# Cross-attention in a decoder layer: how the turned probabilities get from one SBUF tile to another

## The reference

```
h_q = (rmsnorm(layernorm(x)) @ w_q.T).reshape(b, lq, H, DH)
h_k = (ctx @ w_k.T).reshape(b, lk, H, DH)
h_v = (ctx @ w_v.T).reshape(b, lk, H, DH)
score = einsum('bqhd,bkhd->bhqk', h_q, h_k) + position_bias[None]
score = softmax(where(mask, score, -inf)); score = where(mask, score, 0)
attn = einsum('bhqk,bkhd->bqhd', score, h_v).reshape(b, lq, H * DH)
x = layernorm(x)-part + attn @ w_out.T + residual
```

## Time and profile before

| what | value |
|---|---|
| time, median of 3 runs | 1894.92 us |
| the profiled execution's own time | 1894.83 us |
| its span (first to last instruction) | 1893.0 us |
| TensorE busy | 1859.4 us, 98% |
| VectorE, ScalarE, GpSimd busy | 1332.1, 1030.4, 1083.5 us |
| granted clock of TensorE, mean | 0.993 |
| store of xturned, 61 issues | 256 KB each |
| loads of xpraw, 244 issues | 64 KB each |

### The profile page before, as it was taken

One profiled execution on the slowest core, in us unless ns is written; L12 is line 12 of the kernel. 1 busy time (PEld: TensorE's weight loads), 2 busy tenths in 40 slices (PEclk: granted clock), 3 DMA queues, 4 the chain that ended last, 5 costly groups with the idle time before them and its releaser, 6 DMA issues.

```text
span 1893.0 us, 32031 instructions
## 1 busy us (share of the span) xinstructions
PE 1859.4 (98%) x9902; PEld 1598.2 (84%) x9902; DVE 1332.1 (70%) x2212; ACT 1030.4 (54%) x2265; POOL 1083.5 (57%) x861
## 2 busy tenths in 40 slices
PE   9899999999999999998999999999999999999998
PEld 6788888888888888876888888888888888888887
DVE  7688888888888888867666676666666766766132
ACT  3566666666666666655444444444444444445443
POOL 3788888888888888772443443333434434424643
PEclk9999999999999999998999999999999999999999
DMA  7555555555555555641222222222222222212332
GB/s 256 129 126 127 127 127 129 124 127 127 126 128 126 126 126 126 156 128 47 93 87 85 78 83 91 83 70 75 86 91 86 85 85 80 70 55 80 100 121 74
DMA packets 142282, 201.03 MB, mean 106 GB/s; under 512 B 29714, under 2 KB 67218, under 8 KB 141714
## 3 DMA queue, kind: packets, MB, share of 16 engines
q1 hardware_dynamic: 142226, 200.33, 38.0%
HBM read 98.25 MB, written 18.09 MB: 61 GB/s over the span
## 4 chain that ended last, share of the span: by engine, by line
PE 93%; DVE 3%; ACT 2%; issue 1%; SPq 1%; POOL 1%; DMA 0%; DVEq 0%; ACTq 0%
PE bank L1391 25%; PE bank L1392 25%; PE bank L1393 25%; PE bank L1471 11%; PE bank L1616 2%; PE bank L1617 2%; PE bank L1663 2%; PE bank L1664 2%; PE bank L1461 1%; DVE negmax L1012 1%; SPq L295 1%; DVE probT L1020 0%; DVE xacc L1031 0%; ACT prob L657 0%; PE bank L1412 0%
## 5 line engine op out<-in xcount | busy, mean ns | idle before, releaser
L490 POOL TENSOR_TENSOR pT_lo<-pT_lo,pT_hi 128x512 fp32r<-128x512 f32 x320 | 406.3, 1296 | 112.4 <-ACT pT_hi L598 112.4
L1031 DVE SCALAR_TENSOR_TENSOR xacc<-bank,rinv,xacc 128x512 f32<-128x512 f32 x504 | 364.0, 733 | 5.4 <-PE bank L1393 5.4
L657 ACT ACTIVATE prob<-bank,negmax 128x640 f32<-128x640 f32 x256 | 204.0, 797 | 253.1 <-DVE negmax L1012 252.2
L1020 DVE STREAM_TRANSPOSE probT<-prob 128x640 f32<-128x640 f32 x256 | 214.6, 838 | 108.7 <-ACT prob L657 108.7
L1012 DVE TENSOR_REDUCE negmax<-bank 128x1 f32<-128x640 f32 x256 | 207.3, 810 | 39.8 <-PE bank L1471 31.5
L473 POOL TENSOR_TENSOR xwo_lo<-xwo_raw,xwo_hi 128x512 fp32r<-128x512 f32 x32 | 41.5, 1298 | 268.4 <-ACT xwo_hi L598 268.4
L598 ACT ACTIVATE pT_hi<-pT_lo 128x512 fp32r<-128x512 f32 x320 | 185.6, 622 | 3.9 <-DMA pT_lo<-probT 3.9
L473 POOL TENSOR_TENSOR xwq_lo<-xwq_raw,xwq_hi 128x512 fp32r<-128x512 f32 x32 | 41.6, 1299 | 236.5 <-ACT xwq_hi L598 236.5
L1391 PE MATMUL bank<-wx_hi,cT_hi 128*128 128x256 f32 x512 | 142.2, 278 | 1.2 <-DVE xk L1140 1.2
L1393 PE MATMUL bank<-wx_hi,cT_lo 128*128 128x256 f32 x512 | 142.0, 277 | 0.0
L1392 PE MATMUL bank<-wx_lo,cT_hi 128*128 128x256 f32 x512 | 141.9, 277 | 0.0
(11 more groups left out here) (202 smaller groups left out, 5549.1 us busy)
## 6 DMA issues: line engine op xcount, KB each, us to landing
pT_lo<-probT SPq DMA_DIRECT2D x1024, 80.0 KB, 2.1
w_raw<-in_w SPq DMA_DIRECT2D x64, 256.0 KB, 2.8
xturned<-xturn SPq DMA_DIRECT2D x61, 256.0 KB, 2.0
xpraw<-xturned SPq DMA_DIRECT2D x244, 64.0 KB, 2.0
wx_raw<-in_wq SPq DMA_DIRECT2D x32, 256.0 KB, 2.6
wo_raw<-in_wo SPq DMA_DIRECT2D x32, 256.0 KB, 2.7
wx_raw<-in_xwv SPq DMA_DIRECT2D x16, 512.0 KB, 3.3
xwk_raw<-in_xwk SPq DMA_DIRECT2D x32, 256.0 KB, 2.8
```

Of the source, the lines that this page charges most:

```text
L490: g.tensor_tensor(tile, tile.bitcast(F32), four(pT_hi[:, j, :]), ALU.subtract).then_inc(a["pTlo"], 1)
L657: s.activation(prob[:, i % 2, :].rearrange("p (a t) -> p a t", a=2), S_bank[i % 2], ACT.Exp, bias=negmax[:, u % 2, i:i + 1], scale=1.0, ac ...
L1020: v.transpose(probT[:, u % 2, :, :, i * 32:(i + 1) * 32], prob[:, i % 2, :].rearrange("p (t j n) -> p j t n", j=4, n=32)).then_inc(a["turn ...
L1031: v.scalar_tensor_tensor(xacc[:, 4 * half + i, :], M, rinv[:, k, i:i + 1], xacc[:, 4 * half + i, :], ALU.mult, ALU.add).then_inc(sems["y"], 1)
```

## The change

In `c_turn` the store to device memory, the wait for it and the four loads are replaced by 16 transfers straight from xturn to xpraw, one for each block (i, j): 32 partitions, 128 floats (512 bytes) on each. Each adds 16 to the semaphore, so ScalarE waits for 256 (TURN) per unit instead of 64. VectorE, before it overwrites a slot of xturn, waits for the landing of that slot's 16 transfers, where it waited for the store.

```
 def c_turn(it, u):
-    n, use = it * 4 + u, it * 2 + (u + 1) // 2
+    n = it * 4 + u
     sp.wait_ge(c["turned"], n)
     if not isinstance(n, int) or n > 2:
         sp.wait_ge(c["pTlo"], n - 1)
-    sp.dma_start(xturned[u % 2], xturn[:, u % 2].rearrange("p j b q -> p (j b q)")).then_inc(s_xst[u % 2], 16)
-    sp.wait_ge(s_xst[u % 2], use * 16)
-    for j in range(4):
-        sp.dma_start(xpraw[j * 32:(j + 1) * 32, u % 2].rearrange("p i b q -> p i (b q)"),
-                     xturned[u % 2].rearrange("(i k) (j n) -> k i j n", i=4, j=4)[:, :, j, :])\
-          .then_inc(s_xpT[u % 2], 16)
+    for i in range(4):
+        for j in range(4):
+            sp.dma_start(xpraw[j * 32:(j + 1) * 32, u % 2, i],
+                         xturn[i * 32:(i + 1) * 32, u % 2, j]).then_inc(s_xpT[u % 2], 16)
...
 # ScalarE, c_step
-    act.wait_ge(s_xpT[u % 2], (it * 2 + (u + 1) // 2) * 64)
+    act.wait_ge(s_xpT[u % 2], (it * 2 + (u + 1) // 2) * TURN)
...
 # VectorE, c_step
-    dve.wait_ge(s_xst[1 - k], (it * 2 + u // 2) * 16)
+    dve.wait_ge(s_xpT[1 - k], (it * 2 + u // 2) * TURN)
```

## The result

The changed kernel takes 1995.64 us, the median of 3 runs (1994.32 to 1999.83), against 1894.92: a ratio of 1.054, 95% interval 1.052 to 1.056, or +100.7 us. The forecast was 2009 us, slower.

The account below looks back on a forecast made before the run. TensorE, full throughout steady cross-attention, bounds the kernel; afterwards the issue-to-issue loop would: 60 x 14.57 + 30 x 0.49 = 888.9 us against 775.0, +113.9 on 1894.8, taken as 2009 us; overall range 1922 to 2045.

Parts of the forecast that it names:

- The price of an issue: SyncE's queue: 0.59 us per SBUF-to-SBUF transfer, as in the self-attention; last of 16 starts 9.42 us after the first.
- Rivals (1): SyncE issues at the pitch of device-memory loads, 0.48 us: +28, 1923 us; chance 0.10 with prices between.
- (2): Not slower: SyncE issues short rows at 0.35 us or less, TensorE covers it, 1895 us; chance 0.07.
- The landing: Time from a transfer's issue to its data in xpraw: 2.1 us, so data lands 11.5 us after the first issue.
- list of signs: Profile signs; wrong if the set takes under 9 us, landing is not 2.1, or 14.6 us pacing lacks +110 us.
- ring (b): Wait ring through one landing and TensorE's value products: 56.1 us in four units, against 51.92 for TensorE alone.
- (a): Loop between successive sets' first issues, through landing, copy, exponentials and VectorE: 59.3 us in four units, the longest.
- TensorE's idle time: TensorE before the value product, mostly units 1 and 2: about 110 us idle in sum, granted clock still 1.00.
- rival (3): TensorE's clock falls after idle gaps; 5 us of work lost after each of two gives +213, 2108 us; chance 0.05.
- What was costed at nothing: Saved device-memory traffic, VectorE's wait for the landing, SyncE's other queued loads, GpSimd's work: all put at zero.
- Rival (4): SyncE's issue or landing 0.4 us dearer a set: 24 us more, 2033 us; counted within the main case's 0.76.
- The range: Main case 1985 to 2040 us, low end from 0.04 us less per issue; overall 1922 to 2045.

Follow-up runs that it names:

- e8: Changed kernel with 8 of the 16 transfers issued by GpSimd after its bias and mask, the other 8 by SyncE; 1911.31 us, ratio 1.0082.
- e2: Changed kernel with every second block left out, 8 transfers a unit; 1894.49 us, ratio 0.9999.
- e1: Changed kernel without the four diagonal-block transfers, 12 a unit; 1918.89 us, ratio 1.0128.
- e9: Changed kernel with four more 32-row transfers (128 bytes a row, to a scratch tile) behind the 16; 2147.09 us, ratio 1.1333.
- e4: Changed kernel with 14 overwritten 512-column matmuls filling TensorE's gap in unit 2; 1993.53 us, ratio 1.0523.
- e7: Kernel before the change, its store cut into 4 and its 4 loads into 16, still through device memory; 2025.54 us, ratio 1.0692.
- e5: Changed kernel with the copy of xpraw moved from ScalarE to GpSimd, just ahead of its subtraction; 1994.22 us, ratio 1.0524.
- e6: e5 with the 14 matmuls of e4 in TensorE's gap of unit 2; 1971.67 us, ratio 1.0407.
- e3: Changed kernel with ScalarE doing the next unit's exponentials before it waits for the turned probabilities; 1989.57 us, ratio 1.0497.

## Why the prediction was right

- *The price of an issue.* Forecast 0.59 us, a set of 16 in 10.0, from the self-attention's transfers; measured 0.591 and a last issue 9.5 us after the first. Rivals (1) and (2) fell on this. The Trainium skill's page "DMA: Bandwidth & Descriptors", in "Anatomy of one DMA — SWDGE (gpsimd) path", holds that descriptor generation hardly shows beside the completion. It says so of one transfer on GpSimd's path; for a set of small transfers it was the other way round on both queues: GpSimd's eight issues in e8 took 3.93 us beside a landing of 1.7, and SyncE's 15 took 9.5 beside 1.8.
- *The landing.* This is the term that was mis-sized: 2.1 us forecast, from rows of 2560 bytes, 1.8 measured with 512. Over 60 intervals it is 18 us. The intervals were to be 14.57 and 15.06 and are 14.28 to 14.31 and 14.62 to 14.81. Of the 13.2 us between 888.9 and 875.7 the landing explains more than all; the 5 us the other way are in the second and the last turn, 60.1 and 60.3 us where the ring gives 58.1. By the prediction's own list of signs a landing other than 2.1 us counts against it: the path was right and this term of it was not.
- *The loop sets the pace, with ring (b) next under it.* Shown by e2, e1, the changed kernel and e9: eight transfers cost nothing, and each further four 24, 77 and 151 us, as TensorE, then (b), then (a) and again (a) give it to within some us. The prediction had (b) as second longest and used it only for the rivals; without it e1 could not be understood.
- *TensorE's idle time.* Forecast: gaps in units 1 and 2, some 110 us in sum, and a clock that stays. Found: one gap of 3.7 us in unit 2 only, since unit 3's value product comes 17.7 us after unit 2's, not 15.7, and unit 1's gap goes into catching up; about 60 us idle, and 39 us of longer busy time, much of it at the lower clock (15 falls of 1.8 us are 27). This was wrong: the clock that was to stay at 1.00 is 0.96. The clock's fall in rival (3) did come, after a gap shorter than the 4.72 us of the earlier trace rows, so "the gaps are each shorter than that one" was no argument. The rival's 5 us of lost work after a gap came from no row and was 1.8. That a short fall costs nothing was right (e4), for the reason given, the slack of ring (b): 58.1 - 55.8 = 2.3 us.
- *What was costed at nothing*: SyncE's other loads and VectorE's wait. ScalarE's and VectorE's lists of waits name neither, T to T is explained without them, and SyncE's queue is free of loads at 1275.6, 1.3 us before the next set, as forecast.
- Rival (4), dearer sets, did not come.
- *The range.* One of its ends was worked out wrongly: 0.04 us less per issue is 36 us by the prediction's own 9 us for each 0.01, so 1973, not 1985. Nothing hangs on it, as the measured time lies inside either.

## What to carry to other kernels

Before replacing a round trip by many small transfers, write down the ring they stand in: number of issues times the price of one on its queue, plus landing, plus the in-order work until the next set can start, and compare it with the bottleneck's own time for that unit. Up to that point the issues are free. Beyond it each counts as often as its ring passes through a set: once in four units in ring (b) here (8 to 12 transfers, 24 us), in every unit in ring (a) (16 to 20, 151 us). Issuing from a second queue moves the point. A loop's first turns can be off the steady pace, so a steady turn's loss times the number of turns is a little too small (here 92 us of 100.7). When an instruction is moved ahead of a wait to open such a ring, check what the moved instruction waits for itself.

## What the runs showed of the hardware

- SyncE's issue of a 32-partition transfer took 0.591 us with SBUF on both sides, whether rows had 2560, 512 or 128 bytes (2.49 for four of the last), and 0.42 with device memory on one side in the same shape.
- The landing after the issue (medians) shrank with the transfer: from SBUF to SBUF 2.1 us at 80 KB, 1.8 at 16 KB and 1.7 at 4 KB (e9); from device memory 2.0 at 64 KB (before) and 1.7 at 16 KB (e7). Size is not all of it: e7's stores of 64 KB took 1.7.
- GpSimd issued the same transfers at a pitch of 0.49 us (3.93 for eight), landing 1.7 us later, faster than SyncE.
- A like fall of TensorE's clock cost nothing in one kernel (e4, 2 us) and 22.5 us in another (e5 to e6), by whether TensorE was in the ring that set the pace.
- The gaps before such falls were 3.7 us (changed kernel), 4.3 (e5), and in e3 only 1.8 and 1.8, twelve us apart, after which the granted clock was 0.50 from 1273 to 1275 us. In e1, after one gap of 1.2 us that ended at 1291.9, it stayed at 1.00 (1291 to 1299).
